# The second layer norm written by ScalarE instead of GpSimd, with its steps re-ordered around it

## What is computed

```python
def _layernorm(x, axis=-1, eps=1e-05):
    m = jnp.mean(x, axis=axis, keepdims=True)
    v = jnp.var(x, axis=axis, keepdims=True)
    return (x - m) / jnp.sqrt(v + eps)
...
x = L0_attn_x
x = x + _L0_attn_ref(_layernorm(x, axis=-1), ...)
x = x + _L0_ffn_ref(_layernorm(x, axis=-1), ...)
...
# in _L0_ffn_ref
rw = _gating(hidden_states, sim_matrix, gates)     # 16 weights per token, from cosine logits
q = jnp.einsum('bte,bted->btd', rw, jnp.einsum('btc,ecd->bted', hidden_states, q_proj))
# k and v likewise, then causal softmax attention
mixed = attn[:, :, None, :] * rw[..., None]
return jnp.einsum('bted,edc->btc', mixed, o_proj)
```

## Time and profile before

| | us |
|---|---|
| median of three runs | 1405.28 |
| lowest and highest | 1402.79, 1405.67 |
| the profiled execution, timed | 1402.09 |
| its span, first to last instruction | 1400.3 |
| TensorE busy | 1219.1 (87%) |
| VectorE busy | 1183.4 (85%) |
| ScalarE busy | 1119.2 (80%) |
| GpSimd busy | 1060.4 (76%) |

### The profile page before, as it was taken

The page is one execution under the profiler, slowest core; times in us unless marked ns, Lnnn a source line. Parts: engine busy times, 40 slices in busy tenths (PEclk is TensorE's granted clock), DMA queues, the critical chain, the costliest instruction groups (busy, mean ns, idle before and its releaser), DMA issues. The chain is left out here.

```text
span 1400.3 us, 24227 instructions
## 1 busy us (share of the span) xinstructions
PE 1219.1 (87%) x8370; PEld 761.4 (54%) x8370; DVE 1183.4 (85%) x1939; ACT 1119.2 (80%) x2113; POOL 1060.4 (76%) x804
## 2 busy tenths in 40 slices
PE   2789999999999999999999999998855689999997
PEld 1444544445454444454444455444424588889897
DVE  5799999999999999999999999999864576767674
ACT  2799999999999999999999999999954455556553
POOL 2689889899989989998989998899948774535320
PEclk9799999999999999999999999999986899999999
DMA  4232111121211112121111222113005366668570
GB/s 111 66 86 68 37 49 52 31 55 44 64 43 41 52 31 59 41 64 52 31 52 30 60 47 57 31 31 61 1 16 105 72 119 106 120 109 145 101 131 11
DMA packets 184601, 86.88 MB, mean 62 GB/s; under 512 B 150176, under 2 KB 166048, under 8 KB 184480
## 3 DMA queue, kind: packets, MB, share of 16 engines
q1 hardware_dynamic: 184480, 85.33, 28.8%
HBM read 7.68 MB, written 2.10 MB: 7 GB/s over the span
## 5 line engine op out<-in xcount | busy, mean ns | idle before, releaser
L510 POOL TENSOR_TENSOR prob<-prob 128x1024 f32<-128x1024 f32 x255 | 601.7, 2360 | 89.6 <-ACT prob L1156 73.7
L1577 DVE TENSOR_REDUCE negmax<-score_ps 128x1 f32<-128x1024 f32 x512 | 621.2, 1219 | 36.8 <-PE score_ps L756 27.7
L1169 ACT ACTIVATE prob<-score_ps,negmax 128x1024 f32<-128x1024 f32 x512 | 569.7, 1120 | 52.5 <-DVE negmax L1577 47.3
L756 PE MATMUL score_ps<-ka,qa 128*128 128x512 f16 x1024 | 310.1, 385 | 90.1 <-ACT prob L1169 79.6
L779 PE MATMUL trans_ps<-ident,prob 128*128 128x128 f32 x2048 | 269.4, 274 | 2.4 <-POOL prob L510 2.3
L779 PEld LDWEIGHTS trans_ps<-ident,prob 128*128 128x128 f32 x2048 | 239.8, 141 | 56.9 <-POOL prob L510 3.5
L785 PE MATMUL attn_ps<-probT,v_sb 128*64 128x512 f32 x992 | 267.5, 618 | 0.0
L508 POOL TENSOR_SCALAR prob<-prob,ccol 128x1024 f32<-128x1024 f32 x191 | 213.8, 1119 | 2.7 <-DVE ccol L1590 2.7
L562 POOL TENSOR_TENSOR xs<-xnT,rw_all 128x2048 f32<-128x2048 f32 x32 | 119.7, 3740 | 123.4 <-DVE prob L1693 119.9
L756 PEld LDWEIGHTS score_ps<-ka,qa 128*128 128x128 f16 x1024 | 88.9, 98 | 209.5 <-ACT prob L1169 177.6
L348 DVE COPY probT<-trans_ps 128x512 f32<-128x512 f32 x256 | 174.1, 680 | 2.0 <-PE trans_ps L779 2.0
(11 more groups left out here) (246 smaller groups left out, 1387.3 us busy)
## 6 DMA issues: line engine op xcount, KB each, us to landing
qa<-split SPq DMA_DIRECT2D x256, 64.0 KB, 2.0
ka<-split SPq DMA_DIRECT2D x256, 64.0 KB, 2.0
xg<-xnT SPq DMA_DIRECT2D x16, 512.0 KB, 3.0
resid<-in_L_attn_x SPq DMA_DIRECT2D x4, 512.0 KB, 5.6
wg<-in_L_attn_Wkv SPq DMA_DIRECT2D x32, 64.0 KB, 2.0
out<-prob SPq DMA_DIRECT2D x32, 64.0 KB, 2.5
wg<-in_L_attn_Wq SPq DMA_DIRECT2D x16, 64.0 KB, 1.9
xsT<-prob SPq DMA_TRANSPOSE x64, 4.5
```

Source lines behind the costliest of these rows:

```text
L510: pool.tensor_tensor(prob1[:, n % PROBS, :], prob1[:, n % PROBS, :], prob2[:, n % 4, :], ALU.add).then_inc(mix_ok, 1)
L756: mm = pe.matmul(score_ps[:, sub, kh * HALF:(kh + 1) * HALF], qa[:, par, head * 2 + sub, q0:q0 + P], ka[:, par, head * 2 + sub, kh * HALF: ...
L1169: act.activation(prob2[:, n % 4, :] if sub else prob1[:, n % PROBS, :], score_ps[:, sub, :], ACT.Exp, bias=negmax[:, s % 2, sub:sub + 1], ...
L1577: dve.tensor_reduce(negmax[:, s % 2, sub:sub + 1], score_ps[:, sub, :], AX.X, ALU.max, negate=True).then_inc(max_ok, 1)
```

## The change

The write of the normed x moves from GpSimd to ScalarE. GpSimd no longer centres the 1024 columns and no longer scales them; it keeps the variance, the root and one new step of 8 columns, shift = minus the mean times scale. ScalarE writes each of the eight tiles of a batch with one activation, scale times x plus shift, both as pointers to one column (`ln2_normed`). The places of several pieces change with it:

- `ln2_normed(1)` stands in the hand-over, `ln2_normed(2)` in tile 2 between `x_high(4)` and the copy of q and k, `ln2_normed(3)` at the end of tile 8.
- ScalarE's `seed(2)` moves from the end of tile 1 to the middle of it, behind `x_high(3)` and ahead of the copy of q and k; `seed(3)` from the end of tile 6 to the end of tile 7.
- The mean and the squares of batch 3 on ScalarE move from the ends of tiles 3 and 4 to those of tiles 5 and 6; its sum on VectorE from tile 1 to tile 4.
- VectorE's `gate_top(1)` moves ahead of `x_low(3)`.
- On GpSimd the variance of batch 2 comes ahead of `gate_chosen(1)`, that of batch 3 moves from tile 9 to tile 11, and `ln2_scale(3)` from tile 11 to tile 12.

```diff
-            def ln2_centre(b):
+            def ln2_variance(b):
                 pool.wait_ge(g_sq, NT * (b + 1))
-                pool.wait_ge(g_mean, b + 1)
                 pool.tensor_scalar(rows(gs[:, 2, :], b), rows(gs[:, 7, :], b), 1.0 / C, LN_EPS, ALU.mult, ALU.add).then_inc(g_var, 1)
-                pool.tensor_tensor(rows(x2n, b), rows(resid, b), rows(gs[:, 1, :], b).unsqueeze(2).to_broadcast([P, NT, C]),
-                                   ALU.add).then_inc(g_c, 1)
             def ln2_scale(b):
...
                 polished(b, 0, g_scale)
-                t, scale = rows(gs[:, 5, :], b), rows(gs[:, 0, :], b)
+                t, scale, shift = rows(gs[:, 5, :], b), rows(gs[:, 0, :], b), rows(gs[:, 1, :], b)
+                pool.wait_ge(g_mean, b + 1)
+                pool.tensor_tensor(shift, shift, scale, ALU.mult).then_inc(g_c, 1)
...
-                pool.wait_ge(g_c, b)
-                pool.tensor_tensor(rows(x2n, b), rows(x2n, b), scale.unsqueeze(2).to_broadcast([P, NT, C]), ALU.mult).then_inc(g_n, 1)
...
-            ln2_centre(1)
+            ln2_variance(1)
...
                 elif m == 4:
+                    ln2_variance(2)
                     gate_chosen(1)
-                    ln2_centre(2)
...
-                elif m == 9:
-                    ln2_centre(3)
                 elif m == 10:
                     gate_chosen(2)
                 elif m == 11:
-                    ln2_scale(3)
+                    ln2_variance(3)
                 elif m == 12:
                     gate_kept(2)
+                    ln2_scale(3)
...
+            def ln2_normed(b):
+                act.wait_ge(g_scale, b + 1)
+                act.wait_ge(g_c, b)
+                for m in range(b * NT, (b + 1) * NT):
+                    ins = act.activation(x2n[:, m, :], resid[:, m, :], ACT.Identity, scale=gs[:, 0, m:m + 1], bias=gs[:, 1, m:m + 1])
+                ins.then_inc(g_n, 1)
...
             seed(1, g_var, 0)
             root_seed(HALVES - 1)
+            ln2_normed(1)
             seed(1, g_nrm, 2)
...
                 elif m == 1:
                     gate_exp(1)
-                    seed(2, g_var, 0)
                 elif m == 2:
                     seed(2, g_nrm, 2)
                     gate_high(2)
-                elif m == 3:
+                elif m == 5:
                     neg_mean(3)
                     ln2_squares(3 * NT, 3 * NT + 4)
-                elif m == 4:
+                elif m == 6:
                     ln2_squares(3 * NT + 4, 4 * NT)
-                elif m == 6:
-                    seed(3, g_var, 0)
                 elif m == 7:
                     gate_exp(2)
+                    seed(3, g_var, 0)
                 elif m == 8:
+                    ln2_normed(3)
                     seed(3, g_nrm, 2)
...
                         x_high(m + X_AHEAD, t % 2)
+                    if m == 1:
+                        seed(2, g_var, 0)
+                    elif m == 2:
+                        ln2_normed(2)
...
-                elif m == 1:
-                    gate_top(1)
-                    ln2_sum(3)
...
                 elif m == 4:
                     gate_read(2)
+                    ln2_sum(3)
...
+                    if m == 1:
+                        gate_top(1)
                     if not (last and t + X_AHEAD >= NT):
                         x_low(m + X_AHEAD, t % 2)
```

## The result

The changed kernel takes 1408.28 us, the median of nine runs; eight of them lie between 1407.27 and 1412.07, and the ninth, of 4139.08, was in a slow state and is compared with nothing. The kernel before, run beside it, takes 1402.79 (1399.97 to 1405.67). The ratio is 1.0040, 95% interval [1.0026, 1.0054]: slower by 5.6 us (3.6 to 7.6). The forecast was 3.8 us more, and 1409.1. The sign and most of the size are as forecast; the absolute time lies closer than the difference, because the base had stood at 1405.28 and settled at 1402.79. That is luck: a base 2.5 too high made up for a difference some 1.7 too small.

What follows compares the result with a forecast made beforehand. GpSimd's queue bounds up to tile 3, then the loop of ScalarE, VectorE and TensorE in tiles 4 to 9, not TensorE alone. -0.3 - 2.3 + 6.4 = +3.8 us on 1405.28 gives 1409.1, range 1402.5 to 1411.5.

Steps and rivals of the forecast that it cites:

- What bounds the kernel: Hand-over and first ten tiles: GpSimd's queue up to tile 3, then the ScalarE, VectorE, TensorE loop in tiles 4 to 9.
- The rival that the waits of tiles 6 and 9 hide their share: Waits of 2.13 and 1.72 swallow 1.8 and 1.7 of ScalarE's work: +0.3, 1405.6 us; chance 0.11.
- Part 1: Batch 1 in the hand-over: 2.5 us gained on GpSimd, the multiply of tile 4 starting at 73.4 instead of 75.90.
- Part 2: Tiles 1 to 3: nearly all of part 1's gain lost again through GpSimd, x_low and ScalarE waits; parts 1 and 2 together -0.3.
- Both GpSimd rivals: Variance slips past x_low(3): 1407.0 us, chance 0.13; GpSimd's small steps win both places: 1405.0 us, chance 0.10.
- the 5.0 of the sum: Tile 2: TensorE's time from the start of the scores to the end of its experts, taken as 5.0 us.
- the first rival: GpSimd's variance step slips past x_low(3), so seed(2) and all behind come 2.1 earlier: 1407.0 us; chance 0.13.
- The eight activations: ScalarE's write of one batch's norm: 0.47 us each, 0.37 apart, 3.0 for eight, bounds 1.6 and 3.8.
- the lower bound of 1.6: Least cost of eight activations on ScalarE, in us, with pointers free and activations overlapped.
- its rival: The activations cost 1.6; two of three sets stand in loops, so 2.8 less: +1.0, 1406.3 us; chance 0.10.
- Parts 3 and 4: Batch 3's work leaves tiles 4 and 5, -2.3 us, and comes back with its activations in tiles 6 to 9, +6.4.

Runs made afterwards that it cites:

- batch 1 alone: The kernel before with only batch 1 of the norm written by ScalarE, batches 2 and 3 and all places as before: 1398.32 us, 0.9978.
- after's second profile: The changed kernel profiled once more with nothing changed: 1409.41 us.
- the run with the variance first: The changed kernel with GpSimd's variance of batch 2 moved ahead of the multiply of tile 4: 1409.6 us, 1.0054 of the kernel before.
- the squares in the gaps: The changed kernel with batch 3's mean and squares between ScalarE's copy of p2T and exponent in tiles 6 and 7: 1406.91 us, 1.0027.
- batch 3's activations in the gap: The changed kernel with batch 3's eight activations between ScalarE's copy of p2T and exponent in tile 9: 1404.02 us, 1.0021.

## Why the prediction was right, step by step

- *What bounds the kernel* held. ScalarE's work ahead of `x_high` counts one for one (2.75 of 3.04 came back with the activations of batch 3, 1.80 with the first squares), and the same work in the engine's wait is nearly free (0.29 for the activations). The rival that the waits of tiles 6 and 9 hide their share is refuted by these runs.
- *Part 1*, -2.5, measured -2.61, and -2.58 with batch 1 alone.
- *Part 2* went by every link that was worked out, up to the scores of tile 2: the variance held until `x_low` ends, the seed ahead of the copy, the first root step held as well. Both GpSimd rivals needed a step that slips by, and neither did. The size, +2.2, is that of after's second profile (+2.21); its first, and the runs that moved only pieces of batch 3, have +3.05 to +3.36, since TensorE's way from the scores of tile 2 to the transposes took longer than the 5.0 of the sum. The price of the first rival was wrong too: winning that place only moves the block to the next steps, as the run with the variance first shows.
- *The eight activations*: 484 ns each on average over all 24, against 0.47, and 3.18 to 3.19 for eight against 3.0. The estimate of 3.1 by the Trainium skill, ScalarE: Activation LUTs, What ACT_TABLE_LOAD costs, is nearer, and the 484 ns agree with it; the lower bound of 1.6 fell with its rival.
- *Parts 3 and 4* have the right sum for another split, up to tile 8, and that is luck. With the clock held up by idle matmuls, the steps from 5 to 6, 6 to 7 and 7 to 8 are -1.81, -1.51 and +2.76, where I had -0.7, -1.6 and +1.8. VectorE's `ln2_sum(3)`, for which I charged 1.1 in tile 4, is not to be seen there (it stands behind `x_low` of tile 6, so it could lengthen the step from 6 to 7 at the earliest), and about 1.0 more than the squares' 1.80 is lost in the last of these steps. With the squares in the gaps the same step is still 0.95 longer than before, so this is not their price; and TensorE is busy there almost all the time. That points to TensorE's own work, pushed into this step; what share the sum has in it, no run tells.
- *The step that was missing* is TensorE's clock. The prediction has it once, in tile 2 ("coming out of a long wait then as now"), and everywhere else takes matmuls at the speed of the profile before. In tile 9 the scores did not wait before and wait 2.71 in after, and in all six profiles of that order a stretch at the lower level follows, 1.75 to 2.97 us in a step for which the forecast has 0. In tile 2 the way from the scores to the transposes took 5.73 instead of 5.0, and 4.84 in the second profile. In tiles 3 and 6 a stretch costs some 1.6 in one execution and is missing in another. In the first profile the stretches of tiles 3, 6 and 9 make up 5.0 of the 10.0. The difference of the medians, 5.6 against 3.8, is 1.8 above the forecast, about the one stretch of tile 9; but its interval (3.6 to 7.6) holds the forecast as well, so that this stretch is what the forecast lacks in the time is argued and not shown.

## What to carry to other kernels

An operation moved to another engine is priced by its place in the loop, not by its length: the same 3.2 us of activations cost 3.0 ahead of the step that the next engine waits for, and 0.3 in the engine's own wait behind it. Where two engines exclude each other, moving one small step ahead only chose which of them was held; take a step out of that stretch or let nothing urgent stand behind it. Where a move lengthens TensorE's waits, look at the granted clock behind each of them, and take more than one profile before trusting a tile's length.

## What was not expected of the hardware

Stretches of TensorE at the lower granted clock (0.50 to 0.53, 1.2 GHz) cost 1.6 to 3.0 us each. The one of tile 9 follows a wait of 2.7 us in every profile that has it. That of tile 6 comes and goes between executions of one and the same kernel: before has none there in one profile and one in the other. Another, of 1.65 us in the step from `x_high` of tile 16 to that of tile 17, is there in ten of the fourteen profiles and missing in four, and no edit touches that tile:

```profile
1219.00:1222.00 3.00, 3.00 (x19) 2.87 (x18) 2.67 (x3) 1.67 (x4) 2.43 (x8) 0.51 0.50 114
```

That is the window in before, where the step is 12.98; with batch 3's activations in the gap it is 11.32. With some 165 small matmuls that feed nothing, in the waits of tiles 3, 6 and 9, the clock is at 1.00 there and the median 3.2 us lower than without; in tile 9 they fill the wait that the stretch goes with, in tiles 3 and 6 it can be chance. Another 80, in the longest wait, in tile 2, did not keep it up.
